# Moving the once-only weight-feature phase from ahead of sweep 0 to behind its second strip

## What is computed

```python
xn = layernorm(x)                                   # x: 4 x 4096 x 1024
def rfs(z):                                         # random features, R = 1024
    dot = einsum('...d,rd->...r', z, xis[:, None] * proj)
    cor = 0.5 * sum(z * z, -1)[..., None] * xis**2
    return exp(xis) / 32 * exp(dot - cor)
weights = rfs(input_weights)                        # 1024 x 1024, the same for all tokens
s = einsum('bsr,or->bso', rfs(xn), weights)
h = silu(xn @ w1.T * s1) * (xn @ w2.T * s2)         # 1024 -> 4096
h = gelu(h @ h1.T * sh1); h = gelu(h @ h2.T * sh2)  # 4096 -> 4096, twice
out = x + s * silu(h @ w3.T * s3)                   # 4096 -> 1024
```

## Time and profile before

| | us |
|---|---|
| median of the runs shown (2) | 2999.78 |
| the two runs | 2748.84 and 3250.73 |
| the profiled execution | 2746.43 |
| its span on the slowest core (core 7) | 2744.9 |
| spans of the eight cores | 2741.0 to 2744.9 |
| PE busy | 2625.2 (96% of the span) |
| ACT busy / DVE busy / POOL busy | 358.3 / 251.2 / 205.4 |
| granted TensorE clock, mean | 0.988 |

### The profile page before, as it was taken

One profiled execution on the slowest core, in us unless ns is written; L12 is line 12 of the kernel. 1 busy time (PEld: TensorE's weight loads), 2 busy tenths in 40 slices (PEclk: granted clock), 3 DMA queues, 4 the chain that ended last, 5 costly groups with the idle time before them and its releaser, 6 DMA issues.

```text
span 2744.9 us, 28229 instructions; the slowest of 8 cores (2741.0 to 2744.9 us)
## 1 busy us (share of the span) xinstructions
PE 2625.2 (96%) x12054; PEld 1182.4 (43%) x12054; DVE 251.2 (9%) x382; ACT 358.3 (13%) x496; POOL 205.4 (7%) x391
## 2 busy tenths in 40 slices
PE   2799999999999999999999999999999999999995
PEld 1344444444444444444444444444444444444442
DVE  2133000000023200000013300000002200000001
ACT  0212010101022101010121201010102111010100
POOL 1100000000100000000010000000000000000000
PEclk9899999999999999999999999999999999999998
DMA  5388988888886988888897898888888799888882
GB/s 86 53 134 142 156 152 152 152 153 152 152 172 111 156 152 152 153 153 152 152 164 130 133 160 152 152 152 152 152 143 168 128 155 157 153 153 152 152 152 74
DMA packets 67115, 396.25 MB, mean 144 GB/s; under 512 B 7328, under 2 KB 11696, under 8 KB 21936
## 3 DMA queue, kind: packets, MB, share of 16 engines
q0 software_dynamic: 57408, 377.51, 80.5%
q1 hardware_dynamic: 9584, 16.92, 2.3%
HBM read 763.51 MB, written 8.39 MB: 281 GB/s over the span
## 4 chain that ended last, share of the span: by engine, by line
PE 95%; DMA 2%; DVE 1%; ACT 1%; issue 0%; POOL 0%; DVEq 0%; SPq 0%; ACTq 0%; POOLq 0%
PE pb L477 64%; PE pb L504 8%; PE pb L410 8%; PE pb L387 8%; PE pb L440 2%; PE pb L364 2%; DMA g_sb<-iwT 1%; PE pb L335 1%; DMA wring<-w2p 1%; DMA xt_r<-xT 0%; ACT t L517 0%; PE pb L163 0%; PE pb L165 0%; DVE h_sb L298 0%; DVE ln_tmp L200 0%
## 5 line engine op out<-in xcount | busy, mean ns | idle before, releaser
L477 PE MATMUL pb<-h_sb,wring 128*128 128x512 bf16 x4096 | 884.7, 379 | 0.0
L477 PE MATMUL pb<-g_sb,wring 128*128 128x512 bf16 x4096 | 884.7, 379 | 0.0
L477 PEld LDWEIGHTS pb<-h_sb,wring 128*128 128x128 bf16 x4096 | 400.5, 98 | 484.8 <-issue 2.3
L477 PEld LDWEIGHTS pb<-g_sb,wring 128*128 128x128 bf16 x4096 | 400.8, 98 | 483.3
L504 PE MATMUL pb<-h_sb,wring 128*128 128x512 bf16 x1024 | 229.0, 387 | 18.8 <-ACT t L517 18.8
L410 PE MATMUL pb<-xn_fm,wring 128*128 128x512 bf16 x1024 | 233.1, 381 | 2.7 <-DMA wring<-w2p 2.7
L387 PE MATMUL pb<-xn_fm,wring 128*128 128x512 bf16 x1024 | 231.5, 379 | 0.9 <-DMA wring<-w1p 0.9
L524 DVE TENSOR_TENSOR s_sb<-t,s_sb 128x512 f32<-128x512 bf16 x32 | 22.1, 692 | 1968.4 <-ACT t L517 1965.6
L488 ACT ACTIVATE h_sb<-pb,h2s_c 128x512 bf16<-128x512 f32 x128 | 88.0, 687 | 796.1 <-PE pb L477 786.9
L488 ACT ACTIVATE g_sb<-pb,h1s_c 128x512 bf16<-128x512 f32 x128 | 88.0, 687 | 692.9 <-PE pb L477 683.7
L504 PEld LDWEIGHTS pb<-h_sb,wring 128*128 128x128 bf16 x1024 | 101.5, 99 | 145.7 <-issue 29.7
(11 more groups left out here) (71 smaller groups left out, 395.7 us busy)
## 6 DMA issues: line engine op xcount, KB each, us to landing
wring<-h1p POOLq DMA_DIRECT2D x128, 1024.0 KB, 9.9
wring<-h2p POOLq DMA_DIRECT2D x128, 1024.0 KB, 9.8
wring<-w1p POOLq DMA_DIRECT2D x32, 1024.0 KB, 13.8
wring<-w2p POOLq DMA_DIRECT2D x32, 1024.0 KB, 10.8
wring<-w3p POOLq DMA_DIRECT2D x32, 1024.0 KB, 9.8
xt_r<-xT SPq DMA_DIRECT2D x32, 256.0 KB, 4.9
y<-s_sb SPq DMA_DIRECT2D x32, 256.0 KB, 4.7
xt_sweep<-xT POOLq DMA_DIRECT2D x32, 128.0 KB, 12.9
```

Of the source, the lines that this page charges most:

```text
L477: ii = t.matmul(p[quad[og]][:, :], wring[:, slot, k8, og * 128:(og + 1) * 128], src_sb[:, kk * 8 + k8, :], start=(kk == 0 and k8 == 0), st ...
```

## The change

The squares of `iwT` and the whole of `emit_wphase` leave the place ahead of sweep 0. They are emitted inside sweep 0, behind strip 1 and ahead of the 64 matmuls that read `Wt_sb`. The squares now go into the second half of `h_sb` (chunks 16 to 31), which strips 4 to 7 fill later. Since strips 0 and 1 of sweep 0 are now emitted before the sums, their wait for `so_mm` falls away, and strip 2 has it. No DMA is added or taken away, and no arithmetic changes. Behind the change the line numbers of the sweep are 7 lower down to the strips, and 3 higher behind them.

```diff
-        need(v, cast_sem["iwT"], 16)
-        sq_done = 0
-        for j in range(8):
-            sq_done = V(lambda j=j: v.tensor_mul(
-                h_sb[:, 2 * j:2 * j + 2, :].rearrange("p a b -> p (a b)"),
-                iw_c[j], iw_c[j]))
 
         ln2_squares(0, 0)
...
         def emit_wphase():
-            need(t, cV, sq_done)
+            need(t, cV, wstate["sq_done"])
...
-                sqv = h_sb[:, 2 * j:2 * j + 2, :].rearrange("p a b -> p (a b)")
+                sqv = h_sb[:, 16 + 2 * j:18 + 2 * j, :].rearrange("p a b -> p (a b)")
...
         ln2_stats(0)
-        emit_wphase()
         xn_ready_sweep = ln2_bcast_affine(0, 0)
...
                     if s_ == 0:
-                        need(v, cT, wstate["so_mm"])
+                        need(v, cT, wstate.get("so_mm", 0))
...
             ffn1_strip(0)
             ffn1_strip(1)
+
+            if s_ == 0:
+                need(v, cast_sem["iwT"], 16)
+                sqd = 0
+                for j in range(8):
+                    sqd = V(lambda j=j: v.tensor_mul(
+                        h_sb[:, 16 + 2 * j:18 + 2 * j, :].rearrange("p a b -> p (a b)"),
+                        iw_c[j], iw_c[j]))
+                wstate["sq_done"] = sqd
+                emit_wphase()
 
             need(t, cS, feats_done)
             need(t, cS, wstate["wt_done"])
```

## The result

| | us |
|---|---|
| the kernel before, median of 13 runs | 2749.03 |
| the changed kernel, median of 14 runs | 2784.49 (2761.61 to 3195.62) |
| ratio to before | 1.0091, 95% interval 1.0057 to 1.0124 |
| predicted | 2761.4, range 2748 to 2777 |

A forecast was written before the change was run, and what follows sets the result against it. PE was taken to bound the kernel, busy 2625.2 of 2744.9 us; 48.1 us put in behind strip 1 less 33.1 gained at the start added 15.0 to 2746.4, giving 2761.4, range 2748 to 2777.

The forecast's parts named there:

- The start moves ahead by 33.1 us: Ahead of sweep 0, DVE starts on the normalised tokens at 64.9 instead of 97.98 us; all through strip 1 follows.
- the low clock of the spreading matmuls: Ahead of sweep 0, the two spreading matmuls, behind some 9 us of idle PE, take 3.9 us instead of 2.12.
- 48.1 us put in behind strip 1: Behind strip 1 of sweep 0, the moved work stands alone on PE's path and adds 48.1 us.
- each of its five terms: Behind strip 1: wait for squares 8.46, one-column sums 5.87, copies 1.38, 144 matmuls and last Exp 32.0, table load 0.35 us.
- what the sum says: Whole kernel: 48.1 us put in behind strip 1 less 33.1 gained at the start, 15.0 us more.
- A wait of 2.0 us leaves the clock high: Behind the copies' some 1.7 us of idle PE, the 144 matmuls start at the high clock, as after a 2.0 us wait.
- the term of 32.0: Behind strip 1, the 144 matmuls and last Exp take 32.0 us at the high clock; the other bound was 34.0.
- The forecast, 2761.4 with 0.78: Whole kernel: 2761.4 us, 0.5% more than the profiled execution; chance 0.78 for 2755 to 2769.
- The rival of a low clock in the moved phase: Behind strip 1, the 144 and 64 matmuls run 0.43 us apart: 44 us more, 2806 us; chance 0.03.
- Fed better: At strip 0, waits for weights shrink; with lower bounds of sums and spreading matmuls about 9 us, 2752; chance 0.09.
- not slower: In the rest of sweep 0, the earlier start fills 15 us of PE idle time, so no loss; chance 0.04.

The follow-up runs named there:

- the kernel with extra matmuls: The changed kernel with 144 extra matmuls of the same operands, result unused, at the place the phase left: 2794.18 to 2795.81 us, ratio 1.0172 to the kernel before.
- all five sets: The changed kernel, no further edit, run by turns with the kernel before five times: ratios 1.0091, 1.0059, 1.0058, 1.0058 and 1.0068.
- run 18% higher: Not a numbered run: one of the two runs shown of the kernel before, without any edit, at 3250.73 us; the other took 2748.84.
- the first set: The result's own runs of the changed kernel against the kernel before, with its profiled runs: ratio 1.0091; 6 undisturbed, 6 small dips, 4 larger of 16.
- the later sets: Four repeats of the changed kernel, no edit, against the kernel before: ratios 1.0059, 1.0058, 1.0058 and 1.0068; undisturbed runs 2761.79 to 2765.56 us.

## Why the prediction was right and wrong

- *The start moves ahead by 33.1 us.* Right on core 7, from which it was worked out (64.52 against 97.98), and 1.1 us too much on the mean of the eight (32.0): the token squares start 0.2 us earlier on the mean of the cores, and not 1.15, since before the change most cores started them sooner than core 7 did (41.7 to 42.6 us on five, 43.25 on core 7). What was late next was named rightly (the tokens, 41.5 to 43.3 over the cores), and the low clock of the spreading matmuls was paid (2.04 and 1.91 us); the kernel with extra matmuls shows the other price in the same place.
- *48.1 us put in behind strip 1.* Right to 0.5 us on core 4, each of its five terms to 0.6, and to 1.6 us on each of the six cores. The experiments that leave the squares, or all but the matmuls, in place give back what the sum says (2754.0 and 2749.1).
- *A wait of 2.0 us leaves the clock high.* Too simple. The row that I read showed one such wait; in the kernel before, the clock was low behind the same wait at 1522 us. Behind the copies' 1.53 us the first of the 144 matmuls ran at full pitch on core 4, as assumed (4.04 us for two groups of nine); that the term of 32.0 held is in part luck, since no row of before showed this wait.
- *The forecast, 2761.4 with 0.78.* The undisturbed runs of all five sets lie at 2762 to 2766. What failed is the range: the step that set it by how far executions lie apart, for which I took the 3.9 us between cores and the 2.4 us between two agreeing executions. The times before showed a run 18% higher, and I set it aside as a whole instead of asking whether a disturbance can also be small. It can: a pair of cores at a granted clock of 0.81 for 160 us adds 22 us, which is more than the whole effect of the change. I had no term for it, and my upper end of 2777 left it out: half of the first set's runs without a larger disturbance lay near 2785.
- *The rival of a low clock in the moved phase.* It had the right quantity but the wrong level and place. I asked only for 1.2 GHz in the 208 matmuls behind the one-column sums. What came was 0.81, from the features on, across all of it, in some executions. Nothing in the rows of before shows this level.
- *Fed better, or not slower.* Wrong, as their low chances said. The waits for weights came again (1.49 and 2.46 us on core 4), and even their removal gave less than their length.

Of the ratio's 0.91%, 0.54% is the mechanism and the rest the dips. Why dips were so frequent in the first set stays open: the later sets hold 2 of 20 and 4 of 52, and no experiment switched them on or off. The Trainium skill, page TensorE: Matmul & The Clock Gate, section Seeing it yourself, describes a limiter that takes a whole die to 13/16 of the clock while at least three of its cores run dense matmuls, and holds it while the load lasts. The level agrees with the 0.81 here, the extent does not: here two cores of a die were held and two not, the clock came back at 248 us in the middle of the load, and all eight cores of an undisturbed run keep a mean of 0.984 or more.

By the Trainium skill, page ScalarE: Activation LUTs, section What ACT_TABLE_LOAD costs, the change of table would have cost another 1.4 us. The trace has the ACTIVATE right behind a load of 1.28 us, and PE waited 0.41 us for it. ACT had been idle ahead of that load, but where it was busy up to a load there is no further gap either (core 4: ACTIVATE until 788.45, load from 788.52, next ACTIVATE at 789.82): measurement and page differ, and the measurement decides.

## What to carry to other kernels

Work that is done once can be a filler: before moving it off the start, look at what already runs beside it, since at the new place its small helpers (squares on another engine, sums, copies) stand alone on the path. Moving the 144 matmuls away gained nothing. Left at the start, but behind the two spreading matmuls instead of ahead of them, they hid 13 us of DVE work and the first weights, and the kernel was 20 us faster. And where the expected effect is half a per cent, the range must hold what a small disturbance adds, even if no profile yet shows one.

## What the runs showed of the hardware that I had not expected

- A granted clock of 0.81 can hold for a part of an execution and on a part of a die: 86 to 248 us on cores 6 and 7 (matmuls 0.262 us apart: 4.20 us for 16), and in another 84 to some 172 on cores 0 and 1 and 2660 to some 2710 on cores 2 and 3 of the same die. The first two began within 5 us of the clock's rise in the first dense stretch, the third in the middle of a dense stretch.
- The same wait of 2.0 us ahead of one-column matmuls leaves the clock high in one sweep and low in the next (matmuls 0.22 or 0.43 us apart), in one execution on one core. It makes the end of this kernel uncertain by 1.7 us per such wait, and the stretch behind each of ACT's 4.71 us waits takes 28.9 to 30.6 us.
- 1 MB of tokens, first in the queue, landed only at 19 us, with projT and the ring loads asked for right behind it; a ring load of 1 MB lands 6 us behind the one before (130.4 and 136.8 us in the kernel before).
